# Edge attention on one core: steps of two slots, with the accumulator carried through TensorE and ScalarE

## The reference

```python
q = (h @ Wq.T + bq).reshape(N, HEAD_DIM, HEADS) * scaling
k = (h @ Wk.T + bk).reshape(N, HEAD_DIM, HEADS)
v = (h @ Wv.T + bv).reshape(N, HEAD_DIM, HEADS)
s = jnp.einsum('edh,edh->eh', q[row], k[col])
m = jax.ops.segment_max(s, row, num_segments=N)
e = jnp.exp(s - m[row])
z = jax.ops.segment_sum(e, row, num_segments=N)
out = jax.ops.segment_sum((e / z[row])[:, None, :] * v[col], row, num_segments=N)
x = layernorm(x + out.reshape(N, -1) @ Wo.T + bo)
```

## Time and profile before

| | |
|---|---|
| median of 3 runs | 4096.47 us (4023.46 to 4236.0) |
| the profiled execution | 4017.71 us, span 4015.6 us |
| mean granted TensorE clock of the span | 0.743 |
| edge loop: first to last product instruction | 1267.84 to 3715.31 us of the span |
| steps, gathers | 598, 1794 |

### The profile page before, as it was taken

How to read it: one execution, slowest core, us unless ns; L and a number is a source line. 1 busy time by engine, 2 the same in 40 slices (tenths; PEclk the granted TensorE clock), 3 DMA queues, 4 the chain that set the end, 5 groups by cost and what they waited for, 6 DMA issues and landing times. The chain is left out here.

```text
span 4015.6 us, 59591 instructions
## 1 busy us (share of the span) xinstructions
PE 2227.2 (55%) x7109; PEld 1514.8 (38%) x7109; DVE 3211.0 (80%) x8164; ACT 1504.6 (37%) x6480; POOL 2447.6 (61%) x2365
## 2 busy tenths in 40 slices
PE   3999888653002555555555545555555555544776
PEld 3788775432001333333333333333333333323443
DVE  8554467799223999999999999999999999977776
ACT  0110002221001555555555555555555555534332
POOL 3221120003767777777777777777777777765677
PEclk9966568776555788778777787777877778766777
DMA  1211013226513788878887887888777788799222
GB/s 33 64 58 32 16 43 101 89 67 125 171 36 96 231 233 232 232 232 232 231 232 232 232 232 231 232 232 231 232 232 231 232 232 232 229 177 169 80 92 85
DMA packets 329217, 665.86 MB, mean 166 GB/s; under 512 B 63462, under 2 KB 191750, under 8 KB 329016
## 3 DMA queue, kind: packets, MB, share of 16 engines
q0 software_dynamic: 160768, 518.27, 46.4%
q1 hardware_dynamic: 168392, 146.96, 12.7%
HBM read 599.35 MB, written 65.86 MB: 166 GB/s over the span
## 5 line engine op out<-in xcount | busy, mean ns | idle before, releaser
L931 POOL DMA_INDIRECT kv<-kv_rows,idx x1794 | 1863.0, 1038 | 583.7 <-issue 538.5
L1032 PE MATMUL sum_ps<-pv,ident 128*128 128x264 f32 x2392 | 902.0, 512 | 1299.3 <-DVE pv L825 1299.3
L1032 PEld LDWEIGHTS sum_ps<-pv,ident 128*128 128x128 f32 x2392 | 511.3, 237 | 1712.1 <-DVE pv L825 1393.1
L987 ACT ACTIVATE pv<-kv,s 128x33 f32<-128x33 f32 x4784 | 1084.4, 309 | 53.9 <-ACT s L977 27.3
L790 DVE TENSOR_TENSOR prod<-kv,q 128x768 f32<-128x768 f32 x598 | 569.2, 952 | 59.7 <-DMA kv<-kv_rows,idx 59.6
L797 DVE TENSOR_REDUCE s<-prod 128x24 f32<-128x768 f32 x598 | 565.5, 946 | 0.0
L977 ACT ACTIVATE s<-s 128x32 f32<-128x32 f32 x598 | 137.0, 229 | 1126.1 <-DVE s L818 1126.1
L1034 PE MATMUL sum_ps<-pv,ident 128*128 128x264 f32 x1196 | 497.3, 508 | 0.0
L507 PE MATMUL hist_ps<-hot_lo,hot_hi 125*98 125x128 bf16 x1600 | 372.1, 409 | 121.7 <-DVE hot_hi L174 121.7
L825 DVE TENSOR_TENSOR pv<-kv,s 128x528 f32<-128x528 f32 x598 | 417.4, 698 | 0.3 <-ACT s L977 0.3
L507 PEld LDWEIGHTS hist_ps<-hot_lo,hot_hi 125*98 125x98 bf16 x1600 | 370.3, 259 | 123.2 <-issue 68.7
(11 more groups left out here) (164 smaller groups left out, 2450.5 us busy)
## 6 DMA issues: line engine op xcount, KB each, us to landing
q<-q_perm SPq DMA_DIRECT2D x598, 128.0 KB, 3.7
kv<-kv_rows,idx POOLq DMA_INDIRECT x1794, 4.0
kv_rows<-kv_st SPq DMA_DIRECT2D x98, 260.0 KB, 3.0
xt_sb<-in_xT SPq DMA_DIRECT2D x98, 128.0 KB, 3.2
node_rows<-q_st SPq DMA_DIRECT2D x98, 128.0 KB, 3.4
q_perm<-kv_st SPq DMA_DIRECT2D x98, 128.0 KB, 1.9
kv_st<-node_rows,node_id POOLq DMA_INDIRECT x98, 3.1
cols<-edge_keys,run_at POOLq DMA_INDIRECT x98, 2.5
```

The source lines that it names most:

```text
L931: pool.indirect_dma_start(out=kv[:, j, g, :], out_offset=None, in_=kv_rows, in_offset=bass.IndirectOffsetOnAxis(ap=idx[:, j, g:g + 1], axi ...
L987: last = act.activation(pv[:, b, V * VW + at_h:V * VW + at_h + HD + 1], kv[:, j, V, D + at_h:D + at_h + HD + 1], ACT.Copy, scale=s[:, b, V ...
L1032: pe.matmul(sum_ps[b][:, 0:VW], ident[:, :], pv[:, b, g * VW:(g + 1) * VW], start=g == 0, stop=False)
```

## The change

Steps become two slots wide (G = 2, so 849 steps), columns per tile 40, buffers 8, the hardware loop 8 steps. DVE doesn't add the sum to the accumulator any more. `carry` writes the scaled accumulator, as one more operand of 264 floats, into `pv`; PE adds it with a third matmul; ACT copies the whole sum from PSUM back to `acc` (`store`), between the sixth and the seventh head of the next step. The scaling stands last in DVE's step, and waits for the copy of the step before it. The look-up reads the table into a register early in the step, and splits it later (`decode`). ACT's index copy stands at the end of its step. Scratch rows of the table's planning move from `pv` and `prod` into `kv`.

```diff
-G = 3
+G = 2
-C = 39
+C = 40
-U = 6
+U = 8
-B = 6
+BEFORE_STORE = 6
+B = 8
...
-        pv = sb("pv", [P, 2, G * VW])
+        pv = sb("pv", [P, 2, (G + 1) * VW])
...
-                def scale_acc(k, b, tile, first=False):
-
+                def carry(k, b, tile, first=False):
                     if not first:
-                        dve.wait_ge(acc_added, k)
-                    dve.wait_ge(exp_made, k + 1)
...
-                def add_sum(k, b, tile):
-
-                    dve.wait_ge(acc_scaled, k + 1)
-                    dve.wait_ge(summed, k + 1)
-                    at_tile = acc[:, bass.ds(tile * VW, VW)]
-                    dve.tensor_tensor(at_tile, at_tile, sum_ps[b][:, 0:VW], ALU.add).then_inc(acc_added, 1)
+                        dve.wait_ge(acc_stored, k)
+                    dve.tensor_tensor(pv[:, b, G * VW:].rearrange("p (h w) -> p h w", w=HD + 1),
+                                      acc[:, bass.ds(tile * VW, VW)].rearrange("p (h w) -> p h w", w=HD + 1),
+                                      s[:, b, G * HEADS:].unsqueeze(2).to_broadcast([P, HEADS, HD + 1]), ALU.mult).then_inc(carry_made, 1)
...
+                def look_up(k):
+                    dve.reg_mov(entry_r, dve.value_load(step_tab[0:1, bass.ds(k, 1)], min_val=0, max_val=TAB * C * P - 1))
+
+                def decode(b):
+                    v = bounded(dve, entry_r, TAB * C * P - 1)
+                    dve.reg_mov(tile_r[b], v & (P - 1))
+                    dve.reg_mov(col_r[b], v >> PBITS)
...
                     score_sum(k + 1, b1, peeled=peel and j == 0)
+                    look_up(k + 2)
+                    old_maximum(k + 1, b1, tile1, peeled=peel and j == 0)
+                    mask_scores(k + 1, b1, col1)
                     weigh(k, j % U, b, peeled=peel and j < 2)
...
                     maxima(k + 1, b1, tile1)
-                    if before is not None:
-                        add_sum(k - 1, b1, before)
                     if not last:
                         score(k + 2, (j + 2) % U, turn + (j + 2) // U)
-                    scale_acc(k, b, tile, first=peel and j == 0)
+                    decode(b)
                     differences(k + 1, b1, tile1)
...
+                    carry(k, b, tile, first=peel and j == 0)
...
+                    weigh_heads(j, b, range(0, BEFORE_STORE))
+                    if stored:
+                        store(k - 1, 1 - b)
+                    weigh_heads(j, b, range(BEFORE_STORE, HEADS)).then_inc(last_made, 1)
+
+                def store(k, b):
+
+                    v = act.value_load(step_tab[0:1, bass.ds(k, 1)], min_val=0, max_val=TAB * C * P - 1)
+                    tile = bounded(act, v & (P - 1), TILES)
+                    act.wait_ge(summed, k + 1)
+                    act.activation(acc[:, bass.ds(tile * VW, VW)], sum_ps[b][:, 0:VW], ACT.Copy).then_inc(acc_stored, 1)
...
                     pe.wait_ge(last_made, k + 1)
-                    pe.matmul(sum_ps[b][:, 0:VW], ident[:, :], pv[:, b, V * VW:G * VW], start=False, stop=True).then_inc(summed, 1)
...
+                    pe.matmul(sum_ps[b][:, 0:VW], ident[:, :], pv[:, b, V * VW:G * VW], start=False, stop=False)
+                    pe.wait_ge(carry_made, k + 1)
+                    pe.matmul(sum_ps[b][:, 0:VW], ident[:, :], pv[:, b, G * VW:], start=False, stop=True).then_inc(summed, 1)
```

More of the change, by code:

```diff
@@ L798, in score_sum, with old_maximum, mask_scores @@
                                       AX.X, ALU.add).then_inc(scored, 1)
-                def mask_scores(k, b, col, tile):
+                def old_maximum(k, b, tile, peeled=False):
+                    if not peeled:
+                        dve.wait_ge(carry_made, k - 1)
                     dve.tensor_copy(s[:, b, G * HEADS:], runmax[:, bass.ds(tile * HEADS, HEADS)]).then_inc(old_copied, 1)
+                def mask_scores(k, b, col):
                     dve.wait_ge(scored, k + 1)
@@ L846, in _ @@
                 dve.wait_ge(tab_ready, 1)
                 dve.wait_ge(runs_ready, 1)
[L849 to L855, removed]
+                tile_r = [dve.alloc_register(f"tile_{b}") for b in range(2)]
@@ L857, in step @@
+                col_r = [dve.alloc_register(f"col_{b}") for b in range(2)]
+                entry_r = dve.alloc_register("entry")
+                def look_up(k):
[4 more added lines that the diff above has]
+                    dve.reg_mov(col_r[b], v >> PBITS)
                 def step(k, j, turn, peel=False, last=False):
@@ L893, in _ @@
                 weigh(k, k % U, k % 2)
[L894 to L898, removed]
+                carry(k, k % 2, bounded(dve, tile_r[k % 2], TILES))
+                for r in tile_r + col_r + [entry_r]:
                     dve.free_register(r)
@@ L977, in weights, with weigh_heads, weigh_last @@
                     act.activation(s[:, b, :], s[:, b, :], ACT.Exp).then_inc(exp_made, 1)
-                def weigh_last(k, j, turn, b, peeled=False):
+                def weigh_heads(j, b, heads):
+                    for h in heads:
+                        at_h = h * (HD + 1)
+                        last = act.activation(pv[:, b, V * VW + at_h:V * VW + at_h + HD + 1], kv[:, j, V, D + at_h:D + at_h + HD + 1],
+                                              ACT.Copy, scale=s[:, b, V * HEADS + h:V * HEADS + h + 1])
+                    return last
+                def weigh_last(k, j, turn, b, stored=True, peeled=False):
                     act.wait_ge(exp_made, k + 1)
@@ L995, in _ @@
                 weights(0, 0)
-                weigh_last(0, 0, 0, 0, peeled=True)
+                weigh_last(0, 0, 0, 0, stored=False, peeled=True)
                 for k in range(B):
-                    indices(k + U, k % U, 1)
                     weights(k + 1, (k + 1) % 2)
                     weigh_last(k + 1, (k + 1) % U, (k + 1) // U, (k + 1) % 2, peeled=k == 0)
+                    indices(k + U, k % U, 1)
                 with act.Fori(1, LOOPS - 1) as kk:
@@ L1024, in _, with total @@
                 last.then_inc(counts_made, 1)
-                def total(k, b, peeled=False):
+                def total(k, b):
                     pe.wait_ge(pv_made, k + 1)
-                    if not peeled:
-                        pe.wait_ge(acc_added, k - 1)
                     for g in range(V):
@@ L1033, in total @@
                     pe.wait_ge(last_made, k + 1)
-                    pe.matmul(sum_ps[b][:, 0:VW], ident[:, :], pv[:, b, V * VW:G * VW], start=False, stop=True).then_inc(summed, 1)
-                for j in range(B):
-                    total(j, j % 2, peeled=j < 2)
-                with pe.Fori(1, LOOPS) as kk:
+                    pe.matmul(sum_ps[b][:, 0:VW], ident[:, :], pv[:, b, V * VW:G * VW], start=False, stop=False)
+                    pe.wait_ge(carry_made, k + 1)
+                    pe.matmul(sum_ps[b][:, 0:VW], ident[:, :], pv[:, b, G * VW:], start=False, stop=True).then_inc(summed, 1)
+                with pe.Fori(0, LOOPS) as kk:
                     for j in range(B):
```

35 lines of the change are left out of this document (16 added, 19 removed).

## The result

The changed kernel takes 3905.81 us (median of 4 runs, 3892.4 to 3911.78). Against the kernel before, timed on the same chip, the ratio is 0.9699 with a 95% interval of 0.9668 to 0.9731: faster by 3%. The ratio is taken against the two quicker of four runs of the kernel before (4023 and 4026), as the other two, 4096 and 4236, were slow executions. The forecast was 3987, which is 0.9733 of the 4096 that it started from; 109 us less were forecast, and the two profiled runs differ by 4017.71 - 3892.4 = 125.

What follows compares the result with a forecast made beforehand. VectorE bounds before, POOL right behind; afterwards POOL. 559 x 4.02 + 206 = 2453 becomes 813 x 2.72 + 130 + 3 = 2344, 109 us less: 4096 - 109 = 3987 us, range 3840 to 4200.

Steps and rivals of the forecast that it cites:

- POOL becomes the bound, and the holds come on top: Working step after the change: two gathers, 2 x 1.30 = 2.60 us, above VectorE's middle, plus time VectorE holds gathers.
- VectorE bounds by 0.07 us per step: Loop before the change: VectorE fills 3.97 us per step, POOL alone would need 3.90.
- 2.60 + 0.12 = 2.72: Working step after the change: two gathers on POOL plus holds, in us, for 813 steps.
- The mechanism: A VectorE instruction with two SBUF inputs holds a gather that starts in it until it ends; a reduction doesn't.
- the chance figure: Holds if gathers start at chance moments in VectorE's two-input instructions: 0.23 us per step; half, 0.12, was taken.
- look-up 0 to 0.15: VectorE's new step: us the table look-up in two parts may add, hidden or not, within 2.45 to 2.60.
- Under 2.72 by only 0.17: ACT's new step, with the copy from PSUM, takes 2.55 us; costed at nothing while POOL covers it.
- Full clock: TensorE's three matmuls per step: 1.6 us at full clock, 2.9 at half; full was taken.
- Rival (1): TensorE's clock as before, full 58% of the time: step 2.85 us, no change, 4094 us; chance 0.28.
- rival (2): Half clock all the time on TensorE: step 3.05 us, 160 us more, 4256 us; chance 0.22.
- the ring: ACT's copy, two heads, matmuls of last slot and accumulator, and signals wait on each other: 3.05 us at half clock.
- Idle steps: Steps at the loop's end without work: 3.6 us each, 36 of them, 130 us against 206 before.

Runs made afterwards that it cites:

- carry_g3: The changed kernel with steps of three slots instead of two (columns 39, buffers and loop of 6); 4233.85 us, ratio 1.048.
- padded: The changed kernel with one more VectorE reduction, 64 elements of a constant tile, result not used, just before the products; 3853.21 us, ratio 0.956.
- g2_only: The kernel before with two-slot steps alone, buffers and loop of 6, the add still on VectorE; 4712.68 us, ratio 1.1662.
- spread_idle: The changed kernel with the empty tile's indices set to 128 x 40 different rows instead of row 0; 3885.61 us, ratio 0.9638.
- no_mask: The changed kernel without the instruction that adds the mask to the scores; 3961.12 us (one run).
- one_gather: The changed kernel with only the first slot gathered from the ninth step on, the second computing on old rows; 3705.42 us (one run).
- store_first: The changed kernel with ACT's copy of the sum behind the first head instead of the sixth; 4366.48 us (one run).
- run 4023: The kernel before, nothing changed, the fastest of its runs; 4023 us.

## Why the prediction was right

- *Bound.* "POOL becomes the bound, and the holds come on top": shown. POOL has no idle time but issue, and with half of its gathers gone the step falls to 2.52.
- *Bound before.* "VectorE bounds by 0.07 us per step" is not shown. In the kernel before, from 1600 to 3500, VectorE waited for no rows, but POOL had no idle time but issue either, and 3 x (1.032 + 0.305) = 4.01 us of gathers make up the whole step:

```profile
L931 POOL DMA_INDIRECT kv<-kv_rows,idx x1422 | 1467.8, 1032 | 433.5 <-issue 433.5
...
L790 DVE TENSOR_TENSOR prod<-kv,q 128x768 f32<-128x768 f32 x474 | 450.9, 951 | 0.0
```

Both were full, and carry_g3, with the add gone and three slots, was slower. The forecast's sum doesn't rest on that 0.07; it counts POOL's gathers.
- *Step.* Forecast 2.60 + 0.12 = 2.72, measured 2.70 with holds of 0.09: 0.02 x 813 = 16 us too many, which is the difference between 109 and 125. The 3 us for the longer table can't be told: the first product instruction starts at 1267.66 against 1267.84 before, and between 1263.6 and 1269.1 over all versions.
- *Holds.* The mechanism was right. Each gather from 1600 to 3300 was set beside the VectorE instruction that had started last before it and was still running: 144 began in products and lost 36.6 us against 0.998 each, 127 in scaling and lost 9.8, 174 in weigh and lost 8.1; of all others, 376 in the sum among them, none was stretched. For the masks (77) and differences (5) that the forecast also counted, no loss is seen here; in padded 17 of 34 begun in differences are stretched, by 1.8 us in all. That the add held nobody fits g2_only, where 11 gathers begin in it and lose nothing. The size was taken between 0 and 0.42, and the profiled runs show how wide that is: 0.04 (padded), 0.09, 0.125 (spread_idle), 0.18 (no_mask), 0.47 (carry_g3, for three gathers). Halving the chance figure had no reason but its nearness to the steady loop's 0.10, so that the size came out was partly luck.
- *VectorE.* 2.45 to 2.60 forecast, 2.52 for VectorE and ACT together in one_gather. The term "look-up 0 to 0.15" came out at 0.09 in the step shown (pitch 0.69 against 0.60) and at 0.15, its upper end, on the mean of 1600 to 3300 (0.74). What the forecast didn't see is how much hung on the split: undone, the look-up costs 0.63 us per step more. The trace of before showed only the 0.15 that its longer instructions left uncovered.
- *ACT.* "Under 2.72 by only 0.17": 0.23 idle per step are left. The copy is in time, 1.94 us after the differences.
- *TensorE.* Full clock was a choice, and came out: 1.00 in the working steps. Rival (1), the clock of before, and rival (2), the ring at half clock, didn't come about. The ring itself is real: store_first shows it.
- *Idle steps.* 3.6 forecast, 3.67 measured, 73 us saved against the forecast's 76. They are the greater part of the gain.
- *Scale.* The kernel before was put at its first median, 4096; with one more run the median is 4061 and its fastest run 4023, so 3987 lies 2% above the measured 3906 while the ratio differs by 0.003.
- *Not varied.* Eight buffers instead of six were never tried by themselves; POOL waits for none in the kernel before or the changed one.

## What to carry to other kernels

An engine behind the bound isn't free: here VectorE held GpSimd's gathers when a long instruction with two SBUF inputs covered their start, so less work on VectorE went with a slower loop (carry_g3, and no_mask in its one run) and more work with a quicker one (padded), and the phase of the two has to be read from each gather's duration. A fetch into a register that showed 0.15 us behind long instructions showed 0.69 behind short ones: when instructions are shortened, move the fetch forward in the same edit. Padding entries of an index table should point at different rows.

## What the runs showed of the hardware

A table word read by VectorE cost 0.77 us of idle time per step where short instructions stood in front of it, 0.15 behind longer ones. Gathers of 128 times the same row ran at 1.84 us each (3.67 for two), of different rows at 1.34 to 1.37 (2.67 to 2.73 for two). A gather took 1.00 us, and 1.50 when it began 0.06 us after a product instruction of 512 elements; begun in a reduction it was not stretched. An added reduction with a pitch of 0.13 us made the working steps 2% faster each, as the gathers' starts moved out of the products and the holds halved.
